# Local attention layers: a unit's steps stretched over one unit more, a tile's preparation begun one unit sooner

## The reference

```python
for i in range(DEPTH):                                   # 6
    x = attn_layer(shift_tokens(x), Wqkv[i], q_scale[i], k_scale[i], Wo[i]) + x
    x = ffn_layer(shift_tokens(x), ln_g[i], ln_b[i], W1[i], b1[i], W2[i], b2[i]) + x

def attn_layer(x, Wqkv, qs, ksc, Wo):                    # 16 heads of 64
    q, k, v = jnp.split(x @ Wqkv, 3, -1)                 # and into heads
    q = l2norm(q) * qs                                   # t / max(norm(t), 1e-12)
    k = l2norm(k) * ksc
    q = q * cos * scale + rotate_half(q) * sin * scale
    k = k * cos / scale + rotate_half(k) * sin / scale
    out = local_attention(q, k, v)                       # windows of 32 keys: each query
    return out @ Wo                                      # sees itself and 32 before it
```

## Time and profile before

| | |
|---|---|
| median of 3 runs | 5334.38 us (5327.61 to 5336.43) |
| profiled execution | 5326.38 us, span 5324.4 us |
| local layers within it | about 600 to 2390 us |
| mean granted TensorE clock | 0.892 |

### The profile page before, as it was taken

How to read it: one execution, slowest core, us unless ns; L and a number is a source line. 1 busy time by engine, 2 the same in 40 slices (tenths; PEclk the granted TensorE clock), 3 DMA queues, 4 the chain that set the end, 5 groups by cost and what they waited for, 6 DMA issues and landing times. The chain is left out here.

```text
span 5324.4 us, 68492 instructions
## 1 busy us (share of the span) xinstructions
PE 4501.7 (85%) x21823; PEld 2217.4 (42%) x21823; DVE 2850.4 (54%) x3426; ACT 2555.3 (48%) x4400; POOL 2778.0 (52%) x1598
## 2 busy tenths in 40 slices
PE   6988676777777676777986999999999999999983
PEld 2333343443434343442333454444444454545431
DVE  3676463746556463744655555555555555555505
ACT  1544463635446363631452555555555555555540
POOL 0000352635445352520001888888888888888880
PEclk6877798988989898985786999999999999999996
DMA  0000000000000000000001000000000000000000
GB/s 17 3 2 0 33 1 22 1 22 1 17 6 13 10 1 21 1 1 11 1 1 30 2 1 3 3 3 3 3 3 3 3 1 4 2 4 1 1 0 8
DMA packets 18027, 34.97 MB, mean 7 GB/s; under 512 B 3418, under 2 KB 12250, under 8 KB 16746
## 3 DMA queue, kind: packets, MB, share of 16 engines
q1 hardware_dynamic: 17642, 30.22, 1.8%
HBM read 29.69 MB, written 0.52 MB: 6 GB/s over the span
## 5 line engine op out<-in xcount | busy, mean ns | idle before, releaser
L1169 POOL TENSOR_TENSOR xat_p_sum<-xat_p_sum,xat_p_full 128x1024 f32<-128x1024 f32 x768 | 1836.1, 2391 | 227.3 <-ACT xat_p_full L1119 190.9
L1211 DVE TENSOR_REDUCE xat_part<-xat_ring 128x2 f32<-128x1024 f32 (+1 forms) x832 | 951.7, 1181 | 559.1 <-PE xat_ring L989 556.5
L1119 ACT ACTIVATE xat_p_full<-xat_sc 128x512 f32<-128x512 f32 (+1 forms) x1632 | 870.5, 594 | 727.1 <-PE xat_sc L1029 690.8
L1015 PE MATMUL xat_acc<-xat_p_full,xat_v 128*64 128x512 f32 (+1 forms) x3264 | 792.0, 605 | 0.0
L1028 PE MATMUL xat_sc<-xat_q_hh,xat_k_hl 128*128 128x512 f32 (+1 forms) x1632 | 776.1, 476 | 15.4 <-ACT xat_p_full L1119 14.0
L1029 PE MATMUL xat_sc<-xat_q_lm,xat_k_h 128*128 128x512 f32 (+1 forms) x1632 | 645.3, 395 | 0.0
L1706 POOL TENSOR_TENSOR loc_weights_n<-loc_probs,loc_rinv 128x512 f32<-128x512 f32 (+1 forms) x384 | 303.4, 811 | 458.8 <-DVE loc_rinv L1802 307.6
L1690 POOL TENSOR_TENSOR loc_sind<-loc_qk,loc_tab 128x512 f32<-128x512 f32 x192 | 238.9, 1266 | 456.6 <-DVE loc_ss L1746 456.6
L1485 PE MATMUL loc_pr<-loc_w_qkv,loc_xs 128*128 128x512 f32 x576 | 362.6, 763 | 101.1 <-DVE loc_cosd L1753 55.7
L1028 PEld LDWEIGHTS xat_sc<-xat_q_hh,xat_k_hl 128*128 128x128 f32 (+1 forms) x1632 | 303.0, 186 | 301.3 <-issue 155.4
L987 PE MATMUL xat_ring<-xat_k_hl,xat_q_hh 64*128 64x512 f32 (+1 forms) x832 | 332.3, 456 | 29.5 <-DVE xat_part L1211 20.4
(11 more groups left out here) (393 smaller groups left out, 7184.6 us busy)
## 6 DMA issues: line engine op xcount, KB each, us to landing
loc_w_qkv<-in_L_ffn_w SPq DMA_DIRECT2D x6, 1536.0 KB, 7.2
loc_w_o<-in_L_ffn_wo SPq DMA_DIRECT2D x6, 512.0 KB, 3.2
xat_ctxT<-in_ctxT SPq DMA_DIRECT2D x12, 256.0 KB, 2.7
xat_w_qk<-in_L_xattn_wqk SPq DMA_DIRECT2D x16, 128.0 KB, 2.0
loc_w<-in_L_ffn_w SPq DMA_DIRECT2D x6, 341.0 KB, 3.1
loc_w<-in_L_ffn_w SPq DMA_DIRECT2D x6, 192.0 KB, 2.4
loc_rope<-in_rope SPq DMA_DIRECT2D x1, 1024.0 KB
xat_w_o<-in_L_xattn_wo SPq DMA_DIRECT2D x16, 64.0 KB, 1.9
```

What stands on the lines that cost most here:

```text
L1015: last = pe.matmul(acc[h * GROUP:(h + 1) * GROUP, :], v[0:size, t, e * GROUP:(e + 1) * GROUP], p_full[0:size, (e * NT + t) % RING, cols(h) ...
L1119: act.activation(p_full[0:size, at_.buffer(t), cols(h)], sc[0:size, n % 3, :], ACT.Exp, scale=GROUP ** -0.5).then_inc(S["exp_done"], 1)
L1169: pool.tensor_tensor(p_sum[:, e, :], first_in, p_full[:, at_.buffer(t), :], ALU.add)\
L1211: ins = dve.tensor_reduce(part[:, 2 * t:2 * t + 2, c], ring[:, b, :, 0:chunks[c][1]], AX.X, ALU.max)
```

## The change

Nothing is computed otherwise. (1) LEAD = 2: every place of a tile's preparation comes two steps, that is one unit, sooner than before in relation to the units; the loop begins two steps sooner. (2) Within a unit the sum and reciprocal move from step 2x + 1 to 2x + 2, behind the maximum and subtraction of the next unit; the weights from 2x + 1 to 2x + 3; the transposes of P and their copies from 2x + 3 to 2x + 5; the outputs from 2x + 4 to 2x + 7; their copy from 2x + 5 to 2x + 7. (3) On TensorE the outputs stand behind the scores and ahead of the transposes of P, and on ScalarE the copy to att ahead of the copies to pT and pT2. (4) The bound of the norms on VectorE is written as a scalar_tensor_tensor with the same tensor twice.

```diff
+        LEAD = 2
         def preparing(step):
+            step += LEAD
             t = step // NP + 1
...
-        for step in range(-NP - 4, STEPS + 8):
-            if step % 2 and 0 <= step - 3 < STEPS:
+        for step in range(-NP - 4 - LEAD, STEPS + 8):
+            if step % 2 and 0 <= step - 5 < STEPS:
                 for kind in "pe":
-                    tr_at[kind, (step - 3) // 2] = len(tr_at)
+                    tr_at[kind, (step - 5) // 2] = len(tr_at)
...
         def attention(units, prepare):
-            for step in range(-NP - 4, STEPS + 8):
+            for step in range(-NP - 4 - LEAD, STEPS + 8):
...
# TensorE, units(step): behind the scores
-                    x = (step - 3) // 2       # transposes of P
-                    x = (step - 4) // 2       # outputs, even steps
+                    x = (step - 7) // 2       # outputs, odd steps
+                    x = (step - 5) // 2       # transposes of P
# ScalarE, units(step): behind exp
-                    x = (step - 3) // 2       # pT, pT2
-                    x = (step - 5) // 2       # att
+                    x = (step - 7) // 2       # att
+                    x = (step - 5) // 2       # pT, pT2
# GpSimd, units(step)
-                    x = (step - 1) // 2
+                    x = (step - 3) // 2
# VectorE, prepare and units(step)
-                        dve.tensor_scalar(ss[:], ss[:], 1e-12, None, ALU.max).then_inc(S["bound_done"], 1)
+                        dve.scalar_tensor_tensor(out=ss[:], in0=ss[:], scalar=1e-12, in1=ss[:], op0=ALU.max,
+                                                 op1=ALU.max).then_inc(S["bound_done"], 1)
...
-                    x = (step - 1) // 2
-                    if step % 2 and 0 <= x < UNITS:
+                    x = (step - 2) // 2
+                    if step % 2 == 0 and 0 <= x < UNITS:
                         dve.wait_ge(S["exp_done"], i * UNITS + (x + 1))
```

More of the change, by code:

```diff
@@ L1518, in units @@
                         last.then_inc(S["s_ps"], 1)
-                    x = (step - 3) // 2
+                    x = (step - 7) // 2
                     if step % 2 and 0 <= x < UNITS:
[L1521 to L1531, removed]
-                    x = (step - 4) // 2
-                    if step % 2 == 0 and 0 <= x < UNITS:
                         t, u = divmod(x, UN)
@@ L1555, in units @@
                         last.then_inc(S["o_ps"], 1)
+                    x = (step - 5) // 2
+                    if step % 2 and 0 <= x < UNITS:
+                        pe.wait_ge(S["p_done"], i * UNITS + (x + 1))
+                        n = tr_at["p", x]
+                        pe.wait_ge(S["tr_free"], i * (TR * NTOK) + (n - 1))
+                        for c in range(4):
+                            last = pe.transpose(tr[:, n % 2, c * P:(c + 1) * P], weights_n[:, x % 4, c * P:(c + 1) * P],
+                                                g.ident[:])
+                        last.then_inc(S["tr_ps"], 1)
+                        n = tr_at["e", x]
+                        pe.wait_ge(S["tr_free"], i * (TR * NTOK) + (n - 1))
+                        pe.transpose(tr[:, n % 2, 0:P], weights_n[:, x % 4, 4 * P:4 * SPAN], g.ident[:])\
+                          .then_inc(S["tr_ps"], 1)
                 attention(units, prepare)
@@ L1632, in units @@
                         act.activation(probs[:, x % 4, :, :], probs[:, x % 4, :, :], ACT.Exp).then_inc(S["exp_done"], 1)
-                    x = (step - 3) // 2
+                    x = (step - 7) // 2
+                    if step % 2 and 0 <= x < UNITS:
+                        t, u = divmod(x, UN)
+                        act.wait_ge(S["o_ps"], i * UNITS + (x + 1))
+                        act.activation(att[:, 2 * u:2 * u + 2, t * P:(t + 1) * P],
+                                       out_ps[:, :, 0:P],
+                                       ACT.Copy).then_inc(S["o_free"], 1)
+                    x = (step - 5) // 2
                     if step % 2 and 0 <= x < UNITS:
@@ L1642, in units @@
                         act.activation(pT2[:, x % 2, :], tr[:, n % 2, 0:P], ACT.Copy).then_inc(S["tr_free"], 1)
-                    x = (step - 5) // 2
-                    if step % 2 and 0 <= x < UNITS:
[L1645 to L1649, removed]
                 attention(units, prepare)
```

## The result

The changed kernel takes 5347.22 us in the median of 20 runs (5327.89 to 5361.84), the kernel before 5327.73 us (5313.92 to 5346.89, 20 runs). The ratio is 1.0036, with a 95% interval of 1.0023 to 1.0049. A look at each stage says more than the total.

The account below looks back on a forecast made before the run. A loop of waits through the preparation, with no engine full, was taken to bound the kernel; 26.1 + 3.1 = 29.2 us a tile, +8.9 a layer, +53 over six, gave 5379, plus 8 to the median: 5387 us (5355 to 5420).

Parts of the forecast that it names:

- The loop: Local layers: waits through the next tiles' preparation set the pace, 26.1 us a tile at full clock against 25.54.
- The queue: TensorE, k product to q transposes: outputs queued ahead of the P transposes make it about 8.5 us, a loss of 0.7.
- the clock: TensorE in each tile: stretches at half clock (1.2 GHz), 1.6 us each, add 3.1 to 26.1, giving 29.2 us.
- the second place: TensorE's gaps of 0.75 and 2.35 us up to the q transposes: nearly always a low stretch, sometimes twice as long.
- the first place: TensorE's gaps of 1.84 and 0.58 us around the x product: a low stretch in two tiles of three.
- The tail: Last copy of v to output projection: 33.3 us plus a low stretch against 33.5, +1.4 us a layer.
- the first tiles: Start of a layer: first to second copy of v -3.4 us, second to third +0.5 us.
- One place before, two after,: TensorE's gaps that can lower the clock: two places a tile in the new order instead of one.
- The bound: VectorE's bound of the norms: 0.2 us in its new form instead of 1.17, worth nothing to the total.
- The freed loop: Rival: preparation is decoupled and a tile nears TensorE's 19.65 us; at 23 us a tile, 5200 us; chance 0.06.
- One low stretch per tile: Rival: 27.7 us a tile, 5328 us in all; half a stretch more, 5350; chance 0.17.
- Few low stretches: Rival: TensorE's gaps fall where the clock holds, 26.1 us a tile, 5266 us in all; chance 0.15.

Follow-up runs that it names:

- the outputs behind: Changed kernel with TensorE's transposes of P ahead of the outputs, and ScalarE's pT and pT2 copies ahead of att: 5299.52 us, ratio 0.9952.
- hidden: Changed kernel with outputs behind their odd step's preparation, copy to att at the next even step's start: 5301.23 us; that copy behind q's squares too: 5263.72 us.
- both gaps filled: Changed kernel with ten unread products ahead of each x product and ten between the transposes of k and of q: 5273.74 us, ratio 0.9903.
- the half-filled gap: Kernel before with six unread products ahead of each x product, in TensorE's gap of 1.94 us: 5353.35 us, ratio 1.0051.
- the same order: Changed kernel, outputs behind their step's preparation, copy to att behind q's squares: 5263.72 us; with ten unread products between transposes of k and q: 5182.00 us.

## Why the prediction failed in its size

**The loop.** That no engine is full and that the preparation's loop sets the pace was right; pieces (they add up to 26.0 rather than the 26.1 of the forecast), full-clock length (25.98) and the gaps on TensorE, to 0.2 us, came out as worked out. The kernels with other orders bear it out from both sides: 24.60 where the scores no longer wait for qT, 23.60 where the outputs stand nowhere in the loop.

**The queue.** Outputs ahead of the transposes of P: 8.52 us instead of 7.83, right, and borne out by the runs with the outputs behind (8.27) and hidden (a full-clock tile of 23.60 once the copy to att was out of the way too).

**The step that failed is the size of the term "the clock", and with it what I left out of the sum.** The forecast put 3.1 us of low clock on each tile (29.2 us): a stretch at the second place nearly always, sometimes double, one at the first place in two tiles of three, each at "its 1.6 in full". The number of stretches was about right: 1.9 a tile forecast, 56 in 30 tiles measured. The price was not. The mean tile is 28.7 us on a full-clock mean of 26.05, so the low clock costs it 2.6 us, 1.4 a stretch. The 1.6 was read from the kernel before, where the stretch lies around the k product. In the changed kernel only 16 of the 56 lie there; the other 40 lie behind the transposes of q. In a tile with one of each (timeline of the changed kernel, k product, transposes of q, q product):

```profile
1084.39 3.61 PE L1487 MATMUL loc_pr<-loc_w_qkv,loc_xs 128*128 128x512 f32 x4 [0.50 <-ACT loc_v_more L1610]
...
1094.54 1.97 PE L1499 MATMUL loc_tr<-all_ident,loc_cosd 128*128 128x128 f32 x8 [2.18 <-ACT loc_kT L1619]
...
1099.74 1.88 PE L1487 MATMUL loc_pr<-loc_w_qkv,loc_xs 128*128 128x512 f32 x4
```

The first stretch adds 1.63 us (10.15 instead of 8.52), the second 1.35 (5.20 instead of 3.85), and in the tile at 998.50 it is 1.33. So the step "Behind either place ... a low stretch costs its 1.6 in full" held for the first place and not for the second; why the same low time costs less there stays open. Over five tiles and six layers the tiles came out 16 us below the forecast. The tail cost 4 us more and the first tiles, taken together, 1 us less than forecast. That leaves 39 us in the attention of 53.

**Left out:** the forecast put everything but the attention at nothing, on no other ground than that the change doesn't touch it. The rest of a layer came out 1.4 us shorter in the first pair of profiles and 1.5 in the second, 7 us in five places, though its instructions are the same. Windows of TensorE alone over this rest, before and, in the second fence, after:

```profile
1137.15:1196.62 59.47, 43.73 (x104) 0.84 0.07 22
1433.74:1493.79 60.05, 44.36 (x104) 0.81 0.07 21
```

```profile
1450.85:1509.61 58.76, 42.75 (x104) 0.84 0.07 22
```

The same 104 products keep TensorE busy for 1.0 to 1.7 us less, about as much as the rest is shorter, so more of their time ran at full clock; with both gaps filled the same rest took 54.1, 57.3 or 60.5 us in different layers of one kernel. Why the changed kernel gets the better position each time is not shown. Between the 32 and 36 us that the local part then costs in the two pairs of profiles and the 20 of the medians lie differences of the other stages, some 13 to 17 us, that change from one execution to the next; whether the changed kernel gets some of them regularly stays open. Apart from that the forecast started from the median of three runs, 5334, where twenty gave 5328: 7 of the 40 us between 5387 and 5347.

**One place before, two after,** was wrong as I put it. The kernel before has a second weak place, which the half-filled gap brought out: the 0.96 us of which I wrote that alone it does no harm was not alone, with 1.11 ahead of it and 0.76 behind. In the new order both places act in the same tile in 16 of 30 tiles, the one behind the transposes of q in all 30.

**The bound.** I took 0.2 us against the rule of the Trainium skill (VectorE: DVE Perf Modes, "Two Vector instructions with no wait between them") that an instruction with two SBUF inputs also reads through the interface shared with GpSimd. It takes 1.174 us and still ends with GpSimd's sum (997.36 + 1.17 against 996.13 + 2.35). That agrees with the rule, but doesn't show it at work, since the old form, with one tensor read, takes 1.161 and ends there too. The earlier trace rows had shown that end, and my 0.2 rested on nothing. The price of nothing held, as the run with the old bound shows.

**Rivals.** The freed loop is out (25.98 with the clock held). "One low stretch per tile" holds for 8 tiles of 30; its 5350 for half a stretch more lies next to the measured 5347, but by luck, for the tiles have 1.9 stretches and the rest of the difference came from elsewhere. "Few low stretches" is what one gets by filling the gaps, and its price was about right: 5266 forecast for a loop at full clock, 5273.74 measured with the fillers.

## What to carry to other kernels

Lengthening a software pipeline helps only if the stretched steps were in the loop that sets the pace; find the loop first, by one event that comes once a period, and look at what each in-order queue puts ahead of its links. Work that is off the loop belongs in the gaps of its engine and not ahead of a link, on every engine that it touches (here the outputs on TensorE and their copy on ScalarE). And a gap that costs the loop nothing can still be worth closing, for the clock's sake: the same order took 5264 us with its longest gap open and 5182 with useless products in it.

## What the runs showed of the hardware

The low stretches go with gaps in combination: in the kernel before, cutting a gap of 1.94 us to 1.02 only moved the stretch to a place with gaps of 1.11, 0.96 and 0.76 us. One stretch lengthens a tile by 1.35 us (27.33 on 25.98) to 1.7 us (26.30 on 24.60). Within one tile of the changed kernel it was 1.63 us around the k product and 1.35 behind the transposes of q.

Before, one of VectorE's two scalings (of k and q), which read two tensors from SBUF, met GpSimd's weights (2.21 us in the earlier trace rows). Now both do; timeline of the changed kernel:

```profile
1028.92 3.17 DVE L1761 TENSOR_TENSOR loc_cosd<-loc_cosd,loc_ss 128x1024 f32<-128x1024 f32 x2
1029.17 3.19 POOL L1708 TENSOR_TENSOR loc_weights_n<-loc_probs,loc_rinv 128x512 f32<-128x512 f32 x2 [1.99 <-DVE loc_rinv L1805]
...
1034.79 1.40 POOL L1708 TENSOR_TENSOR loc_weights_n<-loc_probs,loc_rinv 128x512 f32<-128x512 f32 x2 [2.43 <-DVE loc_rinv L1805]
```

The two scalings take 3.17 us together where one took 1.20, and the weights 3.19 instead of 1.40. Taken singly, the first scaling takes 1.19 us and the second 2.06, GpSimd's two products 1.85 and 1.38: the first to start isn't slowed, the others are. The full-clock tile came out at 25.98 us, as worked out without a term for this, so here it lies off the loop.
